# State update over all 128 rows, output products directly behind it, gram products and triangle transposes of both heads in one slot each

## The chip, the cores and the metric

The kernel runs on 1 core of one Trainium2 chip. The metric is the device time of a whole launch in microseconds (us), as the median of the runs. The kernel before takes 3196.33 us (3 runs, 3190.98 to 3197.37).

## The reference, cut to what matters

The program is two transformer layers on an input of (8, 512, 256): softmax attention, an FP4-quantized feed-forward layer, a gated delta rule (a linear attention with a state), and a ternary feed-forward layer. A layer norm follows each. The change lies in the gated delta rule alone, with 8 heads of key and value width 128 and chunks of 64 positions:

```python
tri = tril(k_beta @ k.T * decay, -1)              # per chunk, 64 x 64
Tm = solve_triangular(eye + tri, eye, lower=True)
v_new = Tm @ v_beta;  k_cum = Tm @ (k_beta * exp(g))
def step(S, inp):                                 # chunks in order
    attn = where(keep_low, q_i @ k_i.T * dm_i, 0.0)
    v_n = v_i - kc_i @ S
    out = q_i * exp(g_i) @ S + attn @ v_n
    S = S * exp(g_last) + (k_i * exp(g_last - g_i)).T @ v_n
    return S, out
```

q, k and v come from a projection, a causal convolution over 4 positions and SiLU; a gate z multiplies the normed output. What is computed is the same before and after the change.

## The kernel before

The whole of X stays in SBUF. Four stages run one after the other, with a barrier between them. The third, `delta_rule`, takes two heads (e = 0 and 1) of one sequence at a time: a **pair**. There are 8 sequences of 4 pairs, so 32 pairs. A sequence has 512 positions: 4 tiles t of 128 rows, each tile two chunks of 64 (c = 0 and 1), 8 chunks in all (`NCH`).

The order of the work is written out by hand, and it is the same on every engine. While the state of pair q runs through its chunks, the front of pair f = q + 1 is worked in between. Each pair's turn has 9 **slots** n = 0..8 and then 5 levels of the triangular inverse:

- **p1** (TensorE, line 1966): q and k_cum of chunk n times the state S. VectorE then makes v_n in `V2` (line 1743), and ScalarE copies the part for the output (line 1493).
- `front_early(f, n)` on TensorE and on VectorE: a piece of the next pair.
- **ds** (line 1982): k of chunk n times v_n. It waits for `V2` and for ScalarE's copy. VectorE then updates `S` (line 1759; line 1753 in slot 0), and the next slot's p1 waits for that.
- `front_middle(f, n)` (VectorE only), and `front_late(f, n)` on TensorE: another piece of the next pair.
- **oi** (line 1997), in odd slots: the attention rows times v_n of both chunks of a tile. VectorE adds this to the output `O` (line 1771), and runs its own `front_late` after that.

TensorE's pieces of the front are `keys_in`, `values_in` and `queries_in` (projections, line 1828), `gate_in` (1844), `keys_across` (transposes, 1861), `key_gram` (k times k by chunk, 1876) and `lower_across` (transposes of the 64 x 64 triangles, 1896). On VectorE the pieces are the convolution taps (1537), `keys_to_state` (1551), `keys_to_inverse` (1555), `key_norms` (1559 and 1561, waits for key_gram), `lower` (1582, waits for GpSimd's `key_scales`, whose last instruction is line 1339) and `first_level` (1589 and 1591, waits for lower_across). In the pair that follows the end of a sequence VectorE has the statistics of the layer norm in slot 4 too (`statistics`, 1630 and 1633).

After the levels (lines 2008, 2025 and 2030) TensorE runs `query_gram`, and then for each head the products with the inverse: **vk** (line 2051) and **kc** (line 2058).

An operand's rows and columns decide which part of TensorE's array an instruction uses. The profile prints it as 128*128, 64*128 (64 rows, 128 columns), 128*64 or 64*64. p1, the projections and the 128-wide transposes are 128*128; ds is 64*128, since `KK` and `V2` are taken at the 64 rows of one chunk; oi, lower_across, vk and the levels are 64*64; the grams are 128*64; kc is 64*128. An f32 product shows as two LDWEIGHTS and two MATMUL records.

Of the kernel before, what the change touches and what calls it, by code (L numbers as in the profile page):

```python
# [21 lines left out]
P = 128  # L22
B, N, D = 8, 512, 256
TPS = N // P
# [910 lines left out]
def delta_rule(nc, sems, X, C, prep, ffn, W_qkvz, W_ba, conv_w, dt_bias, A_log, norm_weight, W_out):  # L935
# [19 lines left out]
    with ExitStack() as ctx:  # L955
# [224 lines left out]
        NTm, U, L, ZS = ([sb(f"{n}{e}", [P, TPS, CK]) for e in E2] for n in ("NT", "U", "L", "ZS"))  # L1180
        V2, O = [sb(f"V2{e}", [P, TPS, DK]) for e in E2], [sb(f"O{e}", [P, TPS, DK]) for e in E2]
        S = [sb(f"S{e}", [P, DK]) for e in E2]
# [9 lines left out]
        def per_head(*names):  # L1192
# [14 lines left out]
            sem(n) for n in ("rk_step", "rk_done", "rq_step", "rq_done", "fac_step", "fac_done"))  # L1207
        xt_mm, xt_act, xt_dve, op_mm, y_done, st_done, mv_done, eps_done, rstd_done, ln_done = (
            sem(n) for n in ("xt_mm", "xt_act", "xt_dve", "op_mm", "y_done", "st_done", "mv_done", "eps_done", "rstd_done", "ln_done"))

# [45 lines left out]
        def rows(c):  # L1256
            return slice(c * CK, (c + 1) * CK)
# [8 lines left out]
        with nc.Block() as block:  # L1266
# [263 lines left out]
            def _(dve):  # L1530
# [200 lines left out]
                dve.wait_ge(xt_mm, DC)  # L1731
                nc.vector.tensor_copy(xT[:, 1, :], B_[1][:, :]).then_inc(xt_dve, 1)
                for q in range(-1, PAIRS):
                    f = q + 1
                    for n in range(NCH + 1):
                        for e in E2:
                            m = n
                            if has(q) and 1 <= m < NCH:
                                c, t = m % CPT, m // CPT
                                dve.wait_ge(p1_mm[e], q * RS + m)  # L1740
                                if m == 1:
                                    dve.wait_ge(vnc_done[e], q + 1)
                                nc.vector.scalar_tensor_tensor(V2[e][rows(c), t, :], A_[e][rows(c), 0:DK], cneg[q % 2][rows(c), e, t:t + 1],  # L1743
                                                               VV[e][rows(c), t, :], ALU.mult, ALU.add).then_inc(w_done[e], 1)
# [74 lines left out]
            def _(pe):  # L1819
# [97 lines left out]
                def front_early(f, n):  # L1917

                    if n == 0:
                        keys_in(f, 0, 0)  # L1920
                        keys_in(f, 0, 1)
                    if n == 1:
                        gate_in(f, 0, 0)
                    if n == 2:
                        gate_in(f, 1, 0)
                    if n == 3:
                        gate_in(f, 1, 1)
                    if n == 4:
                        key_gram(f, 1)
                    if n == 5:  # L1930
                        values_in(f, 0, 1)
                    if n == 6:
                        values_in(f, 1, 1)
                    if n == 7:
                        lower_across(f, 1)
                    if n == 8:
                        queries_in(f, 0)

                def front_late(f, n):
# [7 lines left out]
                    if n == 3:  # L1947
                        key_gram(f, 0)
                        keys_across(f, 1)
                    if n == 4:  # L1950
                        values_in(f, 0, 0)
                    if n == 5:
                        values_in(f, 1, 0)
                    if n == 6:
                        lower_across(f, 0)

                x_in(0, 0)
                x_in(0, 1)
                for q in range(-1, PAIRS):
                    f = q + 1  # L1960
                    for n in range(NCH + 1):
# [8 lines left out]
                        for e in E2:  # L1970
                            m = n
                            if has(q) and 0 <= m < NCH:
                                c, t = m % CPT, m // CPT
                                if m == 0:
                                    pe.wait_ge(vnc_done[e], q + 1)
                                    pe.wait_ge(kc_done[e], q + 1)
                                    moving = VV[e][rows(c), t, :]
                                else:
                                    pe.wait_ge(w_done[e], q * RS + m)
                                    pe.wait_ge(o1_done[e], q * RS + m)  # L1980
                                    moving = V2[e][rows(c), t, :]
                                nc.tensor.matmul(A_[e][:, DK:2 * DK], KK[e][q % 2][rows(c), t, :], moving, start=True, stop=True).then_inc(ds_mm[e], 1)  # L1982
                        if has(f):
                            front_late(f, n)
                        for e in E2:
                            m = n
                            if has(q) and 0 <= m < NCH and m % CPT == CPT - 1:
# [7 lines left out]
                                for c in range(CPT):  # L1995
                                    source = VV if t == 0 and c == 0 else V2
                                    last = nc.tensor.matmul(B_[e][rows(c), 0:DK], AT[e][q % 2][rows(c), t, :], source[e][rows(c), t, :],  # L1997
                                                            start=True, stop=True)
                                last.then_inc(oi_mm[e], 1)
                    for l in range(1, LEVELS):  # L2000
                        for e in E2:
# [41 lines left out]
                    if has(f):  # L2043
                        query_gram(f, 0)
                        query_gram(f, 1)
                        for e in E2:
                            pe.wait_ge(u_done[e], f * LEVELS + LEVELS)
                            pe.wait_ge(vv_done[e], f + 1)
                            for t in range(TPS):
                                for c in range(CPT):  # L2050
                                    last = nc.tensor.matmul(F0[e][rows(c), t * P:(t + 1) * P], U[e][rows(c), t, :], VV[e][rows(c), t, :],
                                                            start=True, stop=True)
                            last.then_inc(vk_mm[e], 1)
                            pe.wait_ge(at_done[e], f + 1)
                            pe.wait_ge(ssq_done[e], f + 1)
# [338 lines left out]
```

## Time and profile before

| | us |
|---|---|
| median of the runs | 3196.33 (3190.98 to 3197.37) |
| the profiled execution | 3194.53 |
| its span | 3192.8 |
| TensorE (PE) busy | 2971.4 (93%) |
| VectorE (DVE) busy | 2307.4 (72%) |
| ScalarE (ACT) busy | 1235.1 (39%) |
| GpSimd (POOL) busy | 1020.7 (32%) |
| mean granted TensorE clock | 0.965 |

Busy time says how long at least one instruction of an engine was under way. TensorE's matmuls are pipelined and their ends are modelled, so a busy TensorE may still stand still between two of them. The rows of its weight loads (PEld) have starts that are read directly, and the distance between the starts of two groups shows what a group costs.

### The profile page before, as it was taken

How to read it: one execution, taken by the hardware profiler on the slowest of the kernel's cores; microseconds unless marked ns; L12 is line 12 of the kernel's file. 1: busy time of each engine (PE TensorE's matmuls, PEld its weight loads, DVE VectorE, ACT ScalarE, POOL GpSimd, SP SyncE). 2: the span in 40 equal slices, each digit the busy share in tenths (PEclk: the TensorE clock that was granted, in tenths of full speed). 3: DMA queues.
4: the chain of work that ended last, by engine and by line, in shares of the span. 5: the costliest groups of instructions: out<-in, count | busy, mean ns of one | idle time of the engine just before them, and what ended most of it. 6: DMA issues, size and time to landing. Idle time of an engine off the chain costs nothing. (4 is left out here: it accounts for less than half of the span.)

```text
span 3192.8 us, 82005 instructions
## 1 busy us (share of the span) xinstructions
PE 2971.4 (93%) x33019; PEld 2051.3 (64%) x33019; DVE 2307.4 (72%) x5231; ACT 1235.1 (39%) x2975; POOL 1020.7 (32%) x1495
## 2 busy tenths in 40 slices
PE   6999999679997999999999999999999999999897
PEld 3444444246663777777777777777777777777565
DVE  4666677878874788688678678678678678676566
ACT  2433333323334344344344344344344344342354
POOL 3555455527772222222222222132132132121011
PEclk8999999789997999999999999999999999998899
DMA  2121111000001111001001001001001001000000
GB/s 83 36 58 31 32 31 34 22 1 1 1 1 47 32 41 32 22 19 32 22 18 32 21 19 32 19 21 32 19 21 32 19 22 32 18 18 2 4 25 27
DMA packets 94040, 80.43 MB, mean 25 GB/s; under 512 B 54992, under 2 KB 68320, under 8 KB 93664
## 3 DMA queue, kind: packets, MB, share of 16 engines
q1 hardware_dynamic: 93664, 75.18, 8.7%
q8 instruction: 264, 4.33, 0.6%
q14 instruction: 112, 0.92, 0.1%
HBM read 57.70 MB, written 4.85 MB: 20 GB/s over the span
## 5 line engine op out<-in xcount | busy, mean ns | idle before, releaser
L1828 PE MATMUL gd_bk<-gd_xT,gd_wh 128*128 128x512 f32 x768 | 397.3, 627 | 8.9 <-DVE gd_KE L1555 7.4
L480 DVE TENSOR_REDUCE at_nm<-at_ring 128x2 f32<-128x256 f32 (+3 forms) x256 | 199.2, 821 | 142.9 <-PE at_ring L623 142.9
L1537 DVE SCALAR_TENSOR_TENSOR gd_YK<-gd_bk,gd_cw,gd_YK 128x511 f32<-128x511 f32 (+2 forms) x384 | 283.1, 743 | 11.8 <-ACT gd_YK L1406 6.1
L1506 ACT COPY gd_ZS<-gd_bk 128x256 f32<-128x256 f32 x320 | 119.1, 372 | 318.3 <-PE gd_bk L2008 312.3
L2008 PE MATMUL gd_bk<-gd_L,gd_NT 64*64 64x64 f32 x5120 | 203.7, 223 | 26.5 <-DVE gd_L L1597 25.9
L2008 PEld LDWEIGHTS gd_bk<-gd_L,gd_NT 64*64 64x64 f32 x5120 | 169.2, 134 | 78.8 <-DVE gd_L L1597 40.2
L1595 DVE COPY_PREDICATED gd_U<-gd_mU,gd_bk 128x256 f32<-128x256 int32 x320 | 141.0, 442 | 105.5 <-PE gd_bk L2030 75.1
L1493 ACT COPY gd_O<-gd_bk 64x128 f32<-64x128 f32 x448 | 108.5, 259 | 274.8 <-PE gd_bk L1966 273.9
L2025 PE MATMUL gd_bk<-gd_U,gd_ZS 64*64 64x64 f32 x5120 | 207.6, 220 | 0.1
L302 POOL TENSOR_TENSOR at_PT<-at_PT,at_dm 128x1024 f32<-128x1024 f32 (+3 forms) x128 | 197.8, 1545 | 10.6
L2025 PEld LDWEIGHTS gd_bk<-gd_U,gd_ZS 64*64 64x64 f32 x5120 | 174.6, 135 | 40.8 <-issue 37.1
L1828 PEld LDWEIGHTS gd_bk<-gd_xT,gd_wh 128*128 128x128 f32 x768 | 127.5, 192 | 97.6 <-issue 66.1
L1982 PE MATMUL gd_bk<-gd_V,gd_KK 64*128 64x128 f32 x896 | 167.2, 308 | 20.9 <-DVE gd_V L1743 17.8
L561 PE MATMUL at_ring<-at_QT,at_KT 32*128 32x512 f32 (+3 forms) x1024 | 168.7, 504 | 17.6 <-DVE at_PT L452 12.8
L1982 PEld LDWEIGHTS gd_bk<-gd_V,gd_KK 64*128 64x128 f32 x896 | 123.5, 189 | 94.3 <-DVE gd_V L1743 77.5
L2030 PE MATMUL gd_bk<-gd_ZS,gd_U 64*64 64x64 f32 x4096 | 162.0, 218 | 0.0
L1966 PEld LDWEIGHTS gd_bk<-gd_S,gd_PQ 128*128 128x128 f32 x896 | 127.7, 195 | 52.2 <-issue 37.2
L1966 PE MATMUL gd_bk<-gd_S,gd_PQ 128*128 128x128 f32 x896 | 159.4, 302 | 0.0
L336 ACT ACTIVATE at_PT<-at_ring 128x1024 f32<-128x1024 f32 (+3 forms) x128 | 90.1, 704 | 178.7 <-PE at_ring L561 178.7
L1316 POOL TENSOR_TENSOR gd_zz<-gd_zz,gd_nw_row 128x512 f32<-128x512 f32 x64 | 81.3, 1270 | 240.1 <-ACT gd_zz L1426 240.1
L1771 DVE SCALAR_TENSOR_TENSOR gd_O<-gd_O,gd_tab,gd_bk 128x128 f32<-128x128 f32 x256 | 78.2, 344 | 105.8 <-PE gd_bk L1997 105.1
L1743 DVE SCALAR_TENSOR_TENSOR gd_V<-gd_bk,gd_cneg,gd_VV 64x128 f32<-64x128 f32 x448 | 138.0, 346 | 18.4 <-PE gd_bk L1966 15.0
(354 smaller groups left out, 6772.0 us busy)
## 6 DMA issues: line engine op xcount, KB each, us to landing
gd_wh<-in_L_attn_W_qkvz SPq DMA_DIRECT2D x64, 512.0 KB, 3.7
gd_gb<-gates SPq DMA_DIRECT2D x128, 64.0 KB, 3.3
X<-in_L_attn_x SPq DMA_DIRECT2D x8, 512.0 KB, 8.7
at_QT<-at_QS SPq DMA_DIRECT2D x128, 32.0 KB, 2.0
at_KT<-at_KS SPq DMA_DIRECT2D x128, 32.0 KB, 2.0
at_OC<-at_Ob SPq DMA_DIRECT2D x128, 32.0 KB, 2.0
at_RC<-inverse SPq DMA_DIRECT2D x128, 32.0 KB, 1.8
out_x<-X SPq DMA_DIRECT2D x8, 512.0 KB, 2.9
```

The lines of the kernel that those rows point to most:

```text
L302: nc.gpsimd.tensor_tensor(PT[s % RP][:, 2:GH, 0:n], PT[s % RP][:, 2:GH, 0:n], dm[:, 0:n].unsqueeze(1).broadcast_to([P, 2, n]), ALU.mult).t ...
L480: nc.vector.tensor_reduce(nm[v % 2][:, k, c0:c0 + HS + 1:HS], set_of(s, 2 + p)[:, :, 0:n], AX.X, ALU.max).then_inc(max_done, 1)
L561: last_ = nc.tensor.matmul(set_of(s, p)[:, i, 0:n], KT[lane(u)][r, k * P:(k + 1) * P], QT[lane(u)][r, k * P:W], start=True, stop=True)
L1537: nc.vector.scalar_tensor_tensor(out[:, s:W], bank_[:, 0:W - s], cw[:, j, head(f, e), CONVK - 1 - s:CONVK - s], out[:, s:W], ALU.mult, ALU ...
L1595: last = nc.vector.copy_predicated(U[e][:, :, :], wide(mU[l]), chunks(A_[e], 1))
L1743: nc.vector.scalar_tensor_tensor(V2[e][rows(c), t, :], A_[e][rows(c), 0:DK], cneg[q % 2][rows(c), e, t:t + 1], VV[e][rows(c), t, :], ALU.m ...
L1828: ins = nc.tensor.matmul(out[:, :], wh[e][:, k, col * DK:(col + 1) * DK], xT[:, k, :], start=k == 0, stop=k == DC - 1)
L1966: nc.tensor.matmul(A_[e][:, 0:DK], PQ[e][q % 2][:, m // CPT, m % CPT, :, :].rearrange("p s n -> p (s n)"), S[e][:, :], start=True, stop=Tr ...
L1982: nc.tensor.matmul(A_[e][:, DK:2 * DK], KK[e][q % 2][rows(c), t, :], moving, start=True, stop=True).then_inc(ds_mm[e], 1)
L2008: last = nc.tensor.matmul(A_[e][rows(c), t * CK:(t + 1) * CK], NTm[e][rows(c), t, :], L[e][rows(c), t, :], start=True, stop=True)
L2025: last = nc.tensor.matmul(A_[e][rows(c), (TPS + t) * CK:(TPS + t + 1) * CK], ZS[e][rows(c), t, :], U[e][rows(c), t, :], start=True, stop=True)
L2030: last = nc.tensor.matmul(A_[e][rows(c), t * CK:(t + 1) * CK], U[e][rows(c), t, :], ZS[e][rows(c), t, :], start=True, stop=True)
```

## The change

The state update ds is taken over all 128 rows: the stationary operand is all of `KK[:, t, :]`, and the moving one is `V2[:, t % 2, c, :]`, a tile in which chunk c has its own 64 rows and the other 64 hold zeros that are written once at the start. Slot 0 stays as it was in this respect: `rows(c)` of `KK` and of `VV`. So `V2` becomes [128, 2, 2, 128] and is reused every second tile. The output products oi stand directly behind ds, ahead of front_late. key_gram of head 0 moves from slot 3 (late) to slot 4 (early), just ahead of that of head 1; lower_across of head 0 from slot 6 (late) to slot 7 (early). The products with the inverse run vk of both heads first, and then kc of both.

```diff
-        V2, O = [sb(f"V2{e}", [P, TPS, DK]) for e in E2], [sb(f"O{e}", [P, TPS, DK]) for e in E2]
+        V2, O = [sb(f"V2{e}", [P, 2, CPT, DK]) for e in E2], [sb(f"O{e}", [P, TPS, DK]) for e in E2]
...
 (VectorE, once, behind the first copy of xT)
+                for e in E2:
+                    for c in range(CPT):
+                        last = nc.vector.memset(V2[e][rows(1 - c), :, c, :], 0.0)
+                last.then_inc(v2_clear, 1)
...
-                                nc.vector.scalar_tensor_tensor(V2[e][rows(c), t, :], A_[e][rows(c), 0:DK], cneg[q % 2][rows(c), e, t:t + 1],
+                                nc.vector.scalar_tensor_tensor(V2[e][rows(c), t % 2, c, :], A_[e][rows(c), 0:DK], cneg[q % 2][rows(c), e, t:t + 1],
...
 (TensorE, front_early)
                     if n == 4:
+                        key_gram(f, 0)
                         key_gram(f, 1)
...
                     if n == 7:
+                        lower_across(f, 0)
                         lower_across(f, 1)
...
 (TensorE, front_late)
                     if n == 3:
-                        key_gram(f, 0)
                         keys_across(f, 1)
...
-                    if n == 6:
-                        lower_across(f, 0)
...
 (TensorE, ds)
-                                    moving = VV[e][rows(c), t, :]
+                                    fixed, moving = KK[e][q % 2][rows(c), t, :], VV[e][rows(c), t, :]
...
-                                    moving = V2[e][rows(c), t, :]
-                                nc.tensor.matmul(A_[e][:, DK:2 * DK], KK[e][q % 2][rows(c), t, :], moving, start=True, stop=True).then_inc(ds_mm[e], 1)
-                        if has(f):
-                            front_late(f, n)
+                                    if q == 0 and m == 1:
+                                        pe.wait_ge(v2_clear, 1)
+                                    fixed, moving = KK[e][q % 2][:, t, :], V2[e][:, t % 2, c, :]
+                                nc.tensor.matmul(A_[e][:, DK:2 * DK], fixed, moving, start=True, stop=True).then_inc(ds_mm[e], 1)
...
 (TensorE, oi)
-                                    source = VV if t == 0 and c == 0 else V2
-                                    last = nc.tensor.matmul(B_[e][rows(c), 0:DK], AT[e][q % 2][rows(c), t, :], source[e][rows(c), t, :],
+                                    moving = VV[e][rows(c), t, :] if t == 0 and c == 0 else V2[e][rows(c), t % 2, c, :]
+                                    last = nc.tensor.matmul(B_[e][rows(c), 0:DK], AT[e][q % 2][rows(c), t, :], moving,
                                                             start=True, stop=True)
                                 last.then_inc(oi_mm[e], 1)
+                        if has(f):
+                            front_late(f, n)
...
 (TensorE, between vk and kc)
                             last.then_inc(vk_mm[e], 1)
+                        for e in E2:
                             pe.wait_ge(at_done[e], f + 1)
```

## Rows read from the trace of the kernel before

**Rows 1.** Stretch, length, busy PE, PEld, DVE, ACT, POOL (instructions), TensorE clock, DMA.
```profile
1061.00:2935.00 1874.00, 1817.39 (x25765) 1395.36 (x25764) 1425.30 (x3663) 751.86 (x2048) 445.65 (x878) 0.99 0.09 24
```
**Rows 2.** The same for slots 0 to 8 of single pairs, then the last pair.
```profile
2133.03:2162.49 29.46, 28.92 (x218) 19.56 (x216) 22.88 (x66) 15.05 (x45) 9.39 (x19) 1.00 0.01 3
2259.62:2290.70 31.08, 28.93 (x219) 19.57 (x217) 24.47 (x74) 15.06 (x45) 10.60 (x21) 1.00 0.01 2
2018.60:2051.03 32.43, 30.29 (x218) 20.37 (x216) 24.87 (x74) 15.18 (x45) 10.59 (x21) 0.95 0.01 2
2911.63:2932.19 20.56, 19.82 (x89) 14.68 (x87) 12.04 (x35) 6.06 (x28) 0.33 (x2) 0.59 0.00 0
```
**Rows 3.** Timeline of the weight loads (start, length, line, array part) in slots 2 to 4.
```profile
2141.14 0.52 PEld L1966 LDWEIGHTS gd_bk<-gd_S,gd_PQ 128*128 128x128 f32 x4 [0.17 <-issue]
2141.58 0.97 PEld L1844 LDWEIGHTS gd_bk<-gd_wh,gd_xT 128*128 128x128 f32 x8
2142.68 0.52 PEld L1982 LDWEIGHTS gd_bk<-gd_V,gd_KK 64*128 64x128 f32 x4
2143.32 0.42 PEld L1861 LDWEIGHTS gd_bk<-ident,gd_kT 128*128 128x128 f32 x4
2143.79 0.56 PEld L1966 LDWEIGHTS gd_bk<-gd_S,gd_PQ 128*128 128x128 f32 x4
...
2147.20 0.41 PEld L1997 LDWEIGHTS gd_bk<-gd_V,gd_AT 64*64 64x64 f32 x8 [0.17 <-issue]
2147.78 0.52 PEld L1966 LDWEIGHTS gd_bk<-gd_S,gd_PQ 128*128 128x128 f32 x4 [0.17 <-issue]
```
**Rows 4.** The same view, the products with the inverse and the next keys_in.
```profile
2128.91 0.85 PEld L2051 LDWEIGHTS gd_bk<-gd_VV,gd_U 64*64 64x64 f32 x16
2129.93 0.97 PEld L2058 LDWEIGHTS gd_bk<-gd_U,gd_KE 64*128 64x128 f32 x16 [0.17 <-issue]
2130.97 0.85 PEld L2051 LDWEIGHTS gd_bk<-gd_VV,gd_U 64*64 64x64 f32 x16
...
2133.03 0.30 PEld L1828 LDWEIGHTS gd_bk<-gd_xT,gd_wh 128*128 128x128 f32 x2
```
**Rows 5.** Waits within the stage: who waited for whom, us, times, longest.
```profile
PEld gd_bk L1982 <- DVE gd_V L1743: 77.5, 100, 2.6
...
DVE gd_O L1771 <- PE gd_bk L1997: 105.1, 96, 2.3
```
**Rows 6.** Timeline of VectorE and GpSimd in slots 3 to 7 of one pair.
```profile
2147.68 0.61 DVE L1771 SCALAR_TENSOR_TENSOR gd_O<-gd_O,gd_tab,gd_bk 128x128 f32<-128x128 f32 x2 [1.13 <-PE gd_bk L1997]
2148.80 0.59 DVE L1743 SCALAR_TENSOR_TENSOR gd_V<-gd_bk,gd_cneg,gd_VV 64x128 f32<-64x128 f32 x2
2150.10 0.60 DVE L1759 SCALAR_TENSOR_TENSOR gd_S<-gd_S,gd_egl_row,gd_bk 128x128 f32<-128x128 f32 x2
2151.06 0.42 DVE L1561 TENSOR_REDUCE gd_ssk<-gd_DG 128x4 f32<-128x256 f32 x1
2152.09 0.63 DVE L1743 SCALAR_TENSOR_TENSOR gd_V<-gd_bk,gd_cneg,gd_VV 64x128 f32<-64x128 f32 x2
2153.36 0.60 DVE L1759 SCALAR_TENSOR_TENSOR gd_S<-gd_S,gd_egl_row,gd_bk 128x128 f32<-128x128 f32 x2
2154.41 0.20 POOL L1339 TENSOR_SCALAR gd_cneg<-gd_cc 128x8 f32<-128x8 f32 x1
2155.56 0.85 DVE L1582 SCALAR_TENSOR_TENSOR gd_NT<-gd_bk,gd_cneg,gd_gb 128x64 f32<-128x64 f32 x4
2156.33 0.59 DVE L1743 SCALAR_TENSOR_TENSOR gd_V<-gd_bk,gd_cneg,gd_VV 64x128 f32<-64x128 f32 x2
2157.62 0.59 DVE L1759 SCALAR_TENSOR_TENSOR gd_S<-gd_S,gd_egl_row,gd_bk 128x128 f32<-128x128 f32 x2
```
**Rows 7.** Timeline of TensorE in the same slots, wait in brackets.
```profile
2152.51 0.76 PE L1982 MATMUL gd_bk<-gd_V,gd_KK 64*128 64x128 f32 x4 [0.21 <-DVE gd_V L1743]
...
2280.71 0.76 PE L1982 MATMUL gd_bk<-gd_V,gd_KK 64*128 64x128 f32 x4 [1.82 <-DVE gd_V L1743]
```

More of the change, by code:

```diff
@@ L1207, in delta_rule @@
             sem(n) for n in ("rk_step", "rk_done", "rq_step", "rq_done", "fac_step", "fac_done"))
-        xt_mm, xt_act, xt_dve, op_mm, y_done, st_done, mv_done, eps_done, rstd_done, ln_done = (
-            sem(n) for n in ("xt_mm", "xt_act", "xt_dve", "op_mm", "y_done", "st_done", "mv_done", "eps_done", "rstd_done", "ln_done"))
+        xt_mm, xt_act, xt_dve, op_mm, y_done, st_done, mv_done, eps_done, rstd_done, ln_done, v2_clear = (
+            sem(n) for n in ("xt_mm", "xt_act", "xt_dve", "op_mm", "y_done", "st_done", "mv_done", "eps_done", "rstd_done", "ln_done", "v2_clear"))
         w_fc, w_proj = ffn
```

## The prediction

> **What bounds the kernel now.** I read the busy time by stretch first. The stage that the change touches takes 1874 us of the span, and in it TensorE is busy for 97% and VectorE for 76% [rows 1]. Busy TensorE time isn't the same as a working array, so the second view is the start times of its weight loads. In them the reader is to see two kinds of steps. Where one group follows another on the same part of the array, it starts after the time of its own records: p1 (4 records) to gate_in is 0.44 us, keys_across to p1 is 0.47 us, so a 128-column record costs about 0.107 us [rows 3]. Where the part of the array changes, there is more. Gate_in's 8 records are worth 0.86 us and ds starts after 1.10 (0.24 more); ds's 4 records are worth 0.43 us and keys_across starts after 0.64 (0.21 more); oi, whose two chunks run beside each other and which is worth 0.43 too, is followed by p1 after 0.58 (0.15 more) [rows 3]. I call this a **switch** and take 0.2 us for it. The third view is the waits: TensorE's loads wait for V2 77.5 us in all, and VectorE waits 105.1 us for oi [rows 5]. So TensorE bounds the slots, with VectorE's loop over the state close behind it in slots 4 to 7.
>
> **The slots: switches.** I count the changes of array part through slots 0 to 8 of a pair with a front, from the order in the code. Before, ds (64*128) stands between 128*128 work, and oi (64*64) too. By slot 0 to 7 there are 2, 4, 2, 5, 3, 4, 3 and 4 changes, 27 in all. After, ds belongs to the 128*128 work except in slot 0, where it keeps its 64 rows; oi's entry and exit stay; head 0's gram and triangle transposes share the entry and exit of head 1's. That gives 2, 2, 0, 2, 2, 2, 0 and 4, so 14. Thirteen go, at 0.2 us: 2.6 us per pair. ds itself costs the same: p1 loads 128 rows and ds 64, and four records of either are 0.43 us [rows 3].
>
> **The slots: waits.** A wait that goes or comes is worth as much as a switch, so I walk the pair that starts at 2133.03 and takes 29.46 us to the first level [rows 2]. All times are from that start. Up to p1 of slot 4 nothing stops TensorE for more than 0.1 us in such a walk. It started its load at 14.75 and its stream 0.11 later [rows 3]; seven switches (1.4) and head 0's gram (0.43) are gone from ahead of it, so now 13.0. From here on VectorE decides:
> - Slot 4. V2 starts at about 13.6, behind the pieces of slot 3. Key_norms of head 0 now waits for the moved gram: p1 ends at 13.4, switch and 8 pairs of 0.053 bring 14.05, and about 0.2 for the result makes 14.25. Before, VectorE had it at once. S starts 0.8 later, at 15.05. VectorE's next V2 follows S by 1.99 us (2150.10 to 2152.09), so at 17.05, and ds of slot 5 can stream 0.53 us behind that (2152.51 for its load, 0.11 for the load itself), at 17.6 [rows 6, 7]. TensorE is through with p1 and values_in at 17.25: it waits 0.35 us.
> - Slot 5. S comes 1.27 us after V2 [rows 6], at 18.3, and O directly behind it. O no longer waits for oi, since oi now follows ds; that is where VectorE's 105.1 us go [rows 5]. `lower` of head 0 needs GpSimd's scales: they end 3.55 us after the second reduction starts (2151.06 to 2154.61) [rows 6]; this reduction is at 16.0, so 19.6. p1 of slot 6 streams at 19.65.
> - Slot 6. V2 follows `lower` by 0.77 us, at 20.4, S follows V2 by 1.29, at 21.65 [rows 6], and the next p1 streams 0.5 us after S starts, at 22.15. TensorE ended ds at 21.35. Before, lower_across of head 0 stood here and hid this; now 0.8 us are a wait. This is the price of moving it.
> - From p1 of slot 7 to the first level only TensorE counts: p1 0.43, switch, both triangle transposes 0.86, switch, ds 0.43, switch, oi 0.43, switch 0.15, queries_in 0.11 + 1.71, switch: 4.8 us. End at 26.95.
>
> So 29.46 − 26.95 = **2.5 us per pair**, for 31 pairs with both a state loop and a front: 77.5 us. The bounds: with no waits left at all it is 13 x 0.24 = 3.1 us (96 us). With VectorE's steps taken one by one at full length rather than by starts (its records overlap by some hundredths each) I come to 1.7 us (53 us). I take 2.5, since it rests on start-to-start distances.
>
> **vk and kc.** Before, the two heads take 4.12 us from the first vk to keys_in (2128.91 to 2133.03), as vk 1.02 and kc 1.04, twice [rows 4]. Sixteen records of either are worth 0.86. After: 2 x 0.86 + 0.17 + 2 x 0.86 + 0.18 = 3.8 us. kc now waits for all of vk, but what it needs from VectorE (`ssq`) comes at the same time as before or sooner than TensorE gets there. Gain 0.35 us x 32 = 11 us; 0 if a wait fills it.
>
> **What costs nothing.** The four memsets stand on VectorE while TensorE does its first projections; uncovered they'd be about 1 us, once (four times at most 0.3, by rows of like size [rows 6]). The reuse of V2 after two tiles adds no wait, as oi of that tile was issued ahead of the p1 that V2 waits for. The last pair has no front: its chain runs p1, V2, ds, S with TensorE waiting at each step at a clock of 0.59 [rows 2], so a switch is under a wait there; I give it 0, and the first pair, which has no ds, 0 with ±1 us. Queues of SP and GpSimd are passed by nothing.
>
> **The clock.** In pairs behind the end of a sequence VectorE has the statistics in slot 4, and ds of slot 5 waits 1.82 us [rows 7]. These 7 pairs take 31.08 us at a granted clock of 1.00, or 32.43 at 0.95 where it falls (four of the seven fell) [rows 2]. This wait grows by the 0.35 us above less nothing. If all seven fall, 3 x 1.4 = 4 us more; I put 5 us.
>
> **Sum.** 77.5 + 11 − 5 = 84 us. The profiled execution took 3194.5; 3110.7 after. The median is 1.8 us above the profiled one, so **3112 us**, 2.6% faster.
>
> One rule of the skill speaks against the change. Rows 3 show that p1, with 128 rows, starts its four loads 0.11 us apart and gate_in follows at once, so a full-height load is hidden behind the product ahead of it. The Trainium skill (TensorE: Matmul & The Clock Gate, Part 3, The mechanism) says of packed products that a weight load overlaps with running matmuls only where its row group differs; a ds over all 128 rows would differ from nothing. By that rule the loads of ds would show, and rival 3 gives the time; the trace doesn't bear it out.
>
> **Rivals.**
> 1. VectorE's loop bounds more of the slots, and only 1.7 us per pair come: 53 + 11 − 5 = 59 us, **3137**. For it: three waits in a row from slot 4 on hang on it. Against: starts, not lengths, are what the rows give.
> 2. The step of 0.2 us at ds isn't from the array part but from its wait for VectorE, so ds keeps it. Then only the moves of oi, gram and triangles count: 5 switches, 1.0 us, 31 + 11 = 42 us, **3154**. Against: keys_across to p1, where p1 waits for VectorE's S in the same way, has no such step [rows 3].
> 3. A full-height load of ds isn't hidden: 4 x 0.107 = 0.43 us in each of 7 slots, 3.0 us in 31 pairs, 93 us, so **3205**.
> 4. Slower: the clock. TensorE's wait at slot 5 and its new one at slot 6 lie close together, and the clock falls to the lower level (1.2 of 2.4 GHz) in every pair, from ds of slot 5 to the first level. Its stream there is 7.3 us, which doubles; the 0.8 us wait hides a part: 6.5 x 31 = 201 us, **3313**. It decides from 2.5 us a pair on. For it: after 1.82 us of waiting the clock did fall in four of seven. Against: a fall cost 1.35 us (32.43 against 31.08), and the ordinary pairs with their wait of 0.2 us show 1.00 [rows 2, 7]. The Trainium skill (TensorE: Matmul & The Clock Gate, Part 1) has the half clock as the state that idling brings back, which the clock of 0.59 in the last pair agrees with [rows 2].
> 5. More than forecast: the waits at slots 5 and 6 don't come, 96 + 11 = 107, **3089**.
>
> **How the numbers follow.** Forecast 0.60, rival 1 0.19, rival 5 0.09, rival 2 0.06, rival 3 0.03, rival 4 0.03. The range reaches into rivals 1 and 5 and leaves out 2 to 4: 3088 to 3145. About 0.2% (6.4 us) is what a measurement can tell from no change. Faster are the forecast and rivals 1, 2 and 5, 0.94; slower 3 and 4, 0.05, with little between.
>
> **What would show it.** ds in rows as 128*128, and 0.44 us between its load and the next 128*128 group; slots of an ordinary pair in 27.0 us; a new wait of about 0.8 us of p1 for S ahead of slot 7, and 0.3 for V2 at slot 5; hardly any wait of line 1771; vk to keys_in in 3.8 us. Wrong would be a step of 0.64 behind a 128*128 ds, slots over 28 us, or a clock under 0.98 in ordinary pairs.

## The result and the profile after

The changed kernel takes **3104.74 us** (median of 4 runs, 3101.75 to 3115.75) against 3193.65 us for the kernel before, run beside it on the same chips (median of 4). The ratio is **0.9728**, with a 95% interval of 0.97 to 0.9756. The profiled execution took 3101.75 us with a span of 3100.0 us; before it was 3194.53 and 3192.8. The medians are 88.9 us apart and the two profiled executions 92.8 us; I had forecast 84.

Stretches first. The first row is the part of the stage that rows 1 showed, the others are slots 0 to 8 of three pairs: an ordinary one, and two behind the end of a sequence. The columns are as in rows 1.

```profile
1055.00:2842.00 1787.00, 1728.68 (x25789) 1373.19 (x25788) 1429.34 (x3668) 749.19 (x2052) 450.21 (x886) 1.00 0.09 25
2309.64:2336.83 27.19, 26.68 (x218) 19.11 (x216) 23.48 (x67) 15.03 (x45) 9.76 (x21) 1.00 0.01 4
2660.20:2688.77 28.57, 26.68 (x218) 19.11 (x216) 25.14 (x76) 15.08 (x45) 10.95 (x23) 1.00 0.01 3
2200.29:2230.54 30.25, 28.36 (x218) 19.95 (x216) 25.45 (x76) 15.21 (x45) 10.95 (x23) 0.94 0.01 3
```

An ordinary pair's slots went from 29.46 to 27.19 us [rows 2], so 2.27 us less; the forecast said 26.95. VectorE's busy time in them hardly changed (22.88 before, 23.48 now), but it is now 86% of the slots instead of 78%. A pair behind the end of a sequence gained 2.5 us where the clock stayed at 1.00 (28.57 against 31.08 us). Of the seven pairs behind the end of a sequence one shows a fallen clock (0.94) in this execution, where four did before.

The last pair, which has no front beside it, ran at a granted clock of 1.00 this time, 15.45 us against 20.56 at 0.59 before [rows 2]:

```profile
2821.05:2836.50 15.45, 13.40 (x86) 9.65 (x84) 11.04 (x35) 5.95 (x28) 0.43 (x3) 1.00 0.00 1
```

Next the weight loads of TensorE in slots 2 to 4 (start, length, line, part of the array).

```profile
2317.41 0.53 PEld L1968 LDWEIGHTS gd_bk<-gd_S,gd_PQ 128*128 128x128 f32 x4
2317.86 0.97 PEld L1848 LDWEIGHTS gd_bk<-gd_wh,gd_xT 128*128 128x128 f32 x8
2318.76 0.53 PEld L1986 LDWEIGHTS gd_bk<-gd_V,gd_KK 128*128 128x128 f32 x4
2319.20 0.47 PEld L1865 LDWEIGHTS gd_bk<-ident,gd_kT 128*128 128x128 f32 x4
...
2321.71 0.41 PEld L1999 LDWEIGHTS gd_bk<-gd_V,gd_AT 64*64 64x64 f32 x8
2322.29 0.42 PEld L1865 LDWEIGHTS gd_bk<-ident,gd_kT 128*128 128x128 f32 x4 [0.17 <-issue]
2322.68 0.53 PEld L1968 LDWEIGHTS gd_bk<-gd_S,gd_PQ 128*128 128x128 f32 x4
```

ds (line 1986) is 128*128 now. Gate_in's 8 records take 0.90 us to the start of ds instead of 1.10, and ds's 4 records 0.44 us to keys_across instead of 0.64 [rows 3]. Behind oi the 0.58 us stay, as they were before.

The products with the inverse and the next keys_in, same view:

```profile
2359.99 1.72 PEld L2055 LDWEIGHTS gd_bk<-gd_VV,gd_U 64*64 64x64 f32 x32
2361.88 1.86 PEld L2063 LDWEIGHTS gd_bk<-gd_U,gd_KE 64*128 64x128 f32 x32 [0.17 <-issue]
2363.81 0.30 PEld L1832 LDWEIGHTS gd_bk<-gd_xT,gd_wh 128*128 128x128 f32 x2
```

From vk to keys_in it is 3.82 us instead of 4.12 [rows 4].

The waits of the stage (us in total, times, longest). No line for O (now 1775) waiting for oi is left in this view, where 105.1 us stood before [rows 5]. TensorE's loads of ds (1986) wait less for V2, 53.4 us instead of 77.5. Those of p1 (1968) wait more for S, 26.4 us instead of 11.1:

```profile
PEld gd_bk L1986 <- DVE gd_V L1747: 53.4, 69, 2.5
...
PEld gd_bk L1968 <- DVE gd_S L1763: 26.4, 65, 0.7
```

The line of before for p1 is this one:

```profile
PEld gd_bk L1966 <- DVE gd_S L1759: 11.1, 34, 0.3
```

And the walk of slots 4 to 7, for the pair that starts at 2309.64 (all engines, start, length, line):

```profile
2322.37 0.60 DVE L1775 SCALAR_TENSOR_TENSOR gd_O<-gd_O,gd_tab,gd_bk 128x128 f32<-128x128 f32 x2
2322.88 0.68 DVE L1555 TENSOR_TENSOR gd_KE<-gd_bk,gd_tab 128x512 f32<-128x512 f32 x1
2323.48 0.59 DVE L1747 SCALAR_TENSOR_TENSOR gd_V<-gd_bk,gd_cneg,gd_VV 64x128 f32<-64x128 f32 x2
2324.06 0.42 DVE L1559 TENSOR_TENSOR gd_DG<-gd_bk,gd_identc 128x256 f32<-128x256 f32 x1
...
2324.93 0.61 DVE L1763 SCALAR_TENSOR_TENSOR gd_S<-gd_S,gd_egl_row,gd_bk 128x128 f32<-128x128 f32 x2
...
2326.26 1.02 PE L1832 MATMUL gd_bk<-gd_xT,gd_wh 128*128 128x512 f32 x2
2326.94 0.63 DVE L1747 SCALAR_TENSOR_TENSOR gd_V<-gd_bk,gd_cneg,gd_VV 64x128 f32<-64x128 f32 x2
2327.35 0.57 PEld L1986 LDWEIGHTS gd_bk<-gd_V,gd_KK 128*128 128x128 f32 x4 [0.90 <-DVE gd_V L1747]
...
2328.21 0.60 DVE L1763 SCALAR_TENSOR_TENSOR gd_S<-gd_S,gd_egl_row,gd_bk 128x128 f32<-128x128 f32 x2
...
2329.49 0.86 DVE L1582 SCALAR_TENSOR_TENSOR gd_NT<-gd_bk,gd_cneg,gd_gb 128x64 f32<-128x64 f32 x4 [0.17 <-POOL gd_cneg L1339]
...
2330.27 0.59 DVE L1747 SCALAR_TENSOR_TENSOR gd_V<-gd_bk,gd_cneg,gd_VV 64x128 f32<-64x128 f32 x2
...
2331.55 0.59 DVE L1763 SCALAR_TENSOR_TENSOR gd_S<-gd_S,gd_egl_row,gd_bk 128x128 f32<-128x128 f32 x2
2331.94 0.75 PE L1968 MATMUL gd_bk<-gd_S,gd_PQ 128*128 128x128 f32 x4 [0.44 <-DVE gd_S L1763]
```

| from the pair's start, us | forecast | measured |
|---|---|---|
| V2 of slot 4 | 13.6 | 13.84 |
| key_norms of head 0 | 14.25 | 14.42 |
| S of slot 4 | 15.05 | 15.29 |
| V2 of slot 5 | 17.05 | 17.30 |
| S of slot 5 | 18.3 | 18.57 |
| `lower` of head 0 | 19.6 | 19.85 |
| V2 of slot 6 | 20.4 | 20.63 |
| S of slot 6 | 21.65 | 21.91 |
| p1 of slot 7 | 22.15 | 22.30 |
| first level | 26.95 | 27.19 |

The whole error of the walk comes in at V2 of slot 4 and is 0.24 us at the end too. (The forecast for p1 of slot 7 is for its products and the 22.30 is the start of its load, 0.11 us ahead of them; like for like that error is 0.26.) VectorE's own queue sets the start of V2 there: O and KE of slot 3 stand directly ahead of it in the first two lines, with no wait between.

Both waits that the forecast named are there. Values_in starts at 2326.26, its two products are worth 0.85 us (the forecast's 1.71 is for four), and the load of ds starts at 2327.35 and takes 0.11 until it can stream: 0.35 us of wait for V2 at slot 5, as forecast. At slot 7, p1 streams 0.5 us behind S, 22.41 us into the pair, and ds of slot 6, whose products start at 21.25, had ended at 21.68: 0.73 us, where I had 0.8.

### The profile page after: what moved, and what is told of

The parts are those of the page before. It is cut to its first block and busy times, and to the rows that moved or that the text cites. A ratio compares the mean times of both kernels' runs of the same rounds, so it can differ in the third digit from the quotient of the medians.

```text
span 3100.0 us, 82009 instructions
## 1 busy us (share of the span) xinstructions
PE 2875.9 (93%) x33019; PEld 2026.8 (65%) x33019; DVE 2311.7 (75%) x5235; ACT 1230.7 (40%) x2975; POOL 1021.2 (33%) x1495
## 5 line engine op out<-in xcount | busy, mean ns | idle before, releaser
L561 PE MATMUL at_ring<-at_QT,at_KT 32*128 32x512 f32 (+3 forms) x1024 | 167.3, 496 | 18.5 <-DVE at_PT L452 13.6
L1986 PE MATMUL gd_bk<-gd_V,gd_KK 128*128 128x128 f32 x896 | 150.3, 290 | 14.6 <-DVE gd_V L1747 13.0
L1986 PEld LDWEIGHTS gd_bk<-gd_V,gd_KK 128*128 128x128 f32 x896 | 121.5, 190 | 61.2 <-DVE gd_V L1747 53.4
L1968 PE MATMUL gd_bk<-gd_S,gd_PQ 128*128 128x128 f32 x896 | 144.8, 284 | 12.5 <-DVE gd_S L1763 12.5
L299 POOL TENSOR_SCALAR_AFFINE_SELECT at_PT<-at_PT 128x256 f32<-128x256 f32 x128 | 54.6, 427 | 297.8 <-ACT at_PT L336 297.2
L338 ACT ACTIVATE at_PT<-at_PT 128x1024 f32<-128x1024 f32 (+3 forms) x128 | 94.3, 737 | 139.8 <-DVE at_PT L452 139.8
```

What stands on the lines that cost most here:

```text
L561: last_ = nc.tensor.matmul(set_of(s, p)[:, i, 0:n], KT[lane(u)][r, k * P:(k + 1) * P], QT[lane(u)][r, k * P:W], start=True, stop=True)
L1968: nc.tensor.matmul(A_[e][:, 0:DK], PQ[e][q % 2][:, m // CPT, m % CPT, :, :].rearrange("p s n -> p (s n)"), S[e][:, :], start=True, stop=Tr ...
L1986: nc.tensor.matmul(A_[e][:, DK:2 * DK], fixed, moving, start=True, stop=True).then_inc(ds_mm[e], 1)
```

## The experiments

The kernel before ran again beside each variant (medians 3192.35 to 3194.97 us), so times are compared through their ratios to it. Each variant's median is of 4 or 5 runs. "Slots" is the length of slots 0 to 8 of an ordinary pair, read from the profile.

| kernel | slots, us | median, us | ratio (95%) |
|---|---|---|---|
| before | 29.46 | 3193.65 | 1 |
| changed | 27.19 | 3104.74 | 0.9728 (0.97 to 0.9756) |
| e1: changed, ds over 64 rows | 27.78 | 3127.32 | 0.9797 (0.9784 to 0.9811) |
| e2: before, ds over 128 rows alone | 28.93 | 3176.47 | 0.9953 (0.9941 to 0.9966) |
| e3: changed, head 0's triangles back | 26.79 | 3099.02 | 0.9709 (0.9695 to 0.9722) |
| e4: changed, both heads' triangles in slot 6 | 26.99 | 3098.24 | 0.9707 (0.9694 to 0.972) |
| e5: changed, head 0's gram back | 27.37 | 3117.22 | 0.9759 (0.9745 to 0.9773) |
| e6: changed, oi back behind front_late | 28.56 | 3153.92 | 0.9882 (0.9869 to 0.9896) |
| e7: changed, vk and kc by head again | 27.19 | 3122.24 | 0.9764 (0.974 to 0.9789) |
| e8: changed and three edits | 26.40 | 3069.42 | 0.9615 (0.9602 to 0.9628) |
| e9: changed, statistics in slot 8 | 27.19 | 3095.85 | 0.9699 (0.9686 to 0.9713) |
| e10: e6, VectorE's O behind its front_late | 27.76 | 3123.93 | 0.9782 (0.9768 to 0.9795) |
| e12: e8, `lower` of head 1 behind S | 26.46 | 3074.77 | 0.963 (0.9617 to 0.9643) |

**e1: the rows of ds undone.**

```diff
-fixed, moving = KK[e][q % 2][:, t, :], V2[e][:, t % 2, c, :]
+fixed, moving = KK[e][q % 2][rows(c), t, :], V2[e][rows(c), t % 2, c, :]
```

> The changed kernel with one thing undone: ds takes 64 rows again (KK and V2 at the rows of its chunk), everything else as changed. Theory (each change of array part costs 0.2 us): 8 changes more per pair with a front, 1.6 us, of which up to 0.4 lies under the waits at slots 5 and 6: 1.2 to 1.6 us, so an ordinary pair's slots take 28.4 to 28.8 us instead of 27.2, and the time is 37 to 50 us above the changed kernel, about 3142 to 3155. Rival (the step of 0.2 us at ds came from its wait for VectorE): no change, about 3105.

Measured: 22.6 us slower, slots 0.59 us longer, which is less than the 37 to 50 us and the 1.2 to 1.6 us expected. The price of one switch is as forecast. In the weight loads of e1's slot 2, gate_in, ds, keys_across:

```profile
1174.95 0.97 PEld L1848 LDWEIGHTS gd_bk<-gd_wh,gd_xT 128*128 128x128 f32 x8
1176.04 0.52 PEld L1986 LDWEIGHTS gd_bk<-gd_V,gd_KK 64*128 64x128 f32 x4
1176.68 0.42 PEld L1865 LDWEIGHTS gd_bk<-ident,gd_kT 128*128 128x128 f32 x4
```

1.09 and 0.64 us, where the changed kernel has 0.90 and 0.44: the same code, no wait shown in either, only the rows differ. So the shape makes the step, and rival 2 falls. But eight such switches come to 0.59 us, not 1.6. The expectation allowed 0.4 us of cover by waits; at 0.2 us a switch it is about 1.

**e2: the rows of ds alone.** The kernel before with V2, the memsets and the operands of ds as changed, nothing moved.

> The kernel before with one part of the change alone: ds over all 128 rows with the zero-padded V2; order of the work as before. Theory (switches): 9 of the 27 changes of array part go, 1.8 us per pair, 56 us at most; some of it turns into waits for VectorE in slots 4 to 6. 35 to 56 us faster than before: ratio 0.982 to 0.989. Rival (the gain is in the order, oi directly behind ds and the shared slots): under 15 us. Rival (a full-height load is not hidden): slower than before by up to 93 us.

Measured: 0.53 us per pair and a ratio of 0.9953, 15 us (17 by the medians). That misses my 35 to 56 us and lies at the edge of "the gain is in the order". The weight loads of one pair of e2 show where it ends; the first lines are slot 1, the last are slots 4 and 5:

```profile
1176.71 0.52 PEld L1988 LDWEIGHTS gd_bk<-gd_V,gd_KK 128*128 128x128 f32 x4
1177.15 0.97 PEld L1848 LDWEIGHTS gd_bk<-gd_wh,gd_xT 128*128 128x128 f32 x8
...
1186.68 0.56 PEld L1988 LDWEIGHTS gd_bk<-gd_V,gd_KK 128*128 128x128 f32 x4 [0.22 <-DVE gd_V L1747]
...
1187.97 0.57 PEld L1970 LDWEIGHTS gd_bk<-gd_S,gd_PQ 128*128 128x128 f32 x4 [0.52 <-DVE gd_S L1763]
...
1189.99 0.57 PEld L1988 LDWEIGHTS gd_bk<-gd_V,gd_KK 128*128 128x128 f32 x4 [1.22 <-DVE gd_V L1747]
```

ds to gate_in is 0.44 us: a load of full height is hidden as p1's are, and rival 3 falls. ds of slot 3 starts 0.54 us sooner than before in its pair (11.79 against 12.33 us from its start), and this lead never grows again. p1 of slot 3 already waits 0.22 us for S, and from there on what TensorE saves it waits for V2 and S. TensorE's loads wait 107.6 us for the two in the stage of e2 and 88.6 before. VectorE's loop over the state is the second bound, and it was already there: VectorE still stands at O for oi (94.6 us).

**e3 and e4: the triangle transposes.** e3 puts those of head 0 back, e4 puts both heads' into slot 6.

```diff
 (front_early, n == 7)
-                        lower_across(f, 0)
                         lower_across(f, 1)
 (front_late)
+                    if n == 6:
+                        lower_across(f, 0)
```

> The changed kernel with lower_across of head 0 back in slot 6, behind ds. Theory (p1 of slot 7 waits for VectorE's S anyway, so the transposes and their two switches are covered there, and slot 7 is rid of 0.43 us): slots 26.7 us instead of 27.2, 12 to 16 us faster than the changed kernel, about 3090. Rival (only the number of switches counts): one or two switches more, 6 to 12 us slower, about 3114.

> The changed kernel with lower_across of both heads in slot 6, behind ds. Theory: two switches and 0.86 us leave slot 7; in slot 6 head 1's transposes wait for `lower` of head 1 and push p1 of slot 7 by 0.2 us, and ds of slot 7 then waits 0.5 us for V2: net 0.35 to 0.5 us a pair, 11 to 16 us faster than the changed kernel, about 3091. Rival (switch count alone): 2 fewer switches and nothing else, 0.4 us. Rival (the clock falls more often behind the wait at slot 7): slower than the changed kernel.

Measured: 0.40 and 0.20 us a pair less. For e3 that is near the 0.5 expected of the slots: this part of the change costs time. e4 misses its 0.35 to 0.5. The weight loads of e3 in slots 6 and 7:

```profile
1186.28 0.54 PEld L1900 LDWEIGHTS gd_bk<-gd_identc,gd_NT 64*64 64x64 f32 x16
1186.89 0.52 PEld L1969 LDWEIGHTS gd_bk<-gd_S,gd_PQ 128*128 128x128 f32 x4
1187.53 0.55 PEld L1900 LDWEIGHTS gd_bk<-gd_identc,gd_NT 64*64 64x64 f32 x16
1188.15 0.53 PEld L1987 LDWEIGHTS gd_bk<-gd_V,gd_KK 128*128 128x128 f32 x4
```

p1 of slot 7 starts 22.39 us into its pair against 22.30 in the changed kernel: the transposes and both their switches fit into the time for which p1 waited for S anyway. ds of slot 7 comes 1.26 us behind it instead of 1.75. In e4 there is more in that place than the wait can hide:

```profile
1190.04 0.52 PEld L1970 LDWEIGHTS gd_bk<-gd_S,gd_PQ 128*128 128x128 f32 x4
1190.98 0.57 PEld L1988 LDWEIGHTS gd_bk<-gd_V,gd_KK 128*128 128x128 f32 x4 [0.42 <-DVE gd_V L1747]
```

p1 of slot 7 starts 22.86 us into its pair, 0.57 later than in the changed kernel and not the 0.2 I expected, and ds behind it waits 0.42 us for V2.

As times, both are only 6 to 7 us faster than the changed kernel, and the intervals overlap. For e4, 31 x 0.2 makes that; for e3 31 x 0.4 would make 12. Its pairs behind the end of a sequence gained only 0.17 us (28.40 against 28.57). In e3's profile three of them take 30.0 us and not 28.4, where the changed kernel's has one such pair, and these two more are 3.3 us of it.

**e5: the gram of head 0 back in slot 3.**

```diff
 (front_early, n == 4)
-                        key_gram(f, 0)
                         key_gram(f, 1)
 (front_late, n == 3)
+                        key_gram(f, 0)
                         keys_across(f, 1)
```

> The changed kernel with key_gram of head 0 back in slot 3, behind oi and ahead of keys_across. Theory (VectorE's loop decides slots 4 to 6, and key_norms of head 0 would no longer wait, but p1 of slot 4 comes 0.6 us later and V2 with it): S of slot 4 0.3 us later, slots 27.5 us, 9 us slower than the changed kernel. Rival (switches alone, one more of 0.17 us, under no wait): 5 us slower. Rival (the moved gram delays VectorE more than it saves): faster than the changed kernel.

Measured: slots 27.37, so 0.18 us and 5.6 us in 31 pairs. That size lies by the rival's 5 us rather than by my 9. The path is nearer to what I expected: V2 of slot 4 waits for p1 and comes 14.18 us into the pair instead of 13.84, S of slot 4 comes 0.20 us later, and so does all that follows.

```profile
1180.78 0.60 DVE L1747 SCALAR_TENSOR_TENSOR gd_V<-gd_bk,gd_cneg,gd_VV 64x128 f32<-64x128 f32 x2 [0.26 <-PE gd_bk L1968]
```

The time is 10 us by the ratios; five of its seven pairs behind the end of a sequence show the fallen clock, four more than the changed kernel's one.

**e6: oi back behind front_late.** The switches stay the same in number.

```diff
                                 nc.tensor.matmul(A_[e][:, DK:2 * DK], fixed, moving, start=True, stop=True).then_inc(ds_mm[e], 1)
+                        if has(f):
+                            front_late(f, n)
...
                                 last.then_inc(oi_mm[e], 1)
-                        if has(f):
-                            front_late(f, n)
```

> The changed kernel with oi back behind front_late; the number of changes of array part stays the same as in the changed kernel. Theory (VectorE's queue stands at O until oi, and its loop over S is delayed by it in slots 1, 3 and 5): the waits of VectorE for oi come back to 60 us or more, and slots take 27.6 to 28.2 us instead of 27.2, 13 to 30 us slower. Rival (only switches count): no change within 3 us.

Measured: 1.37 us a pair and 49 us. This is the largest part of the change, and more than the 13 to 30 us expected. The waits of VectorE in e6's stage bring back 69.8 us for O:

```profile
DVE gd_O L1775 <- PE gd_bk L2001: 69.8, 97, 2.3
```

**e10: the same, but VectorE's update of O moved too.** e6 with `front_late(f, n)` ahead of the update of O in VectorE's block; TensorE's order is e6's.

> The kernel with oi back behind front_late (28.57 us for the slots, 3154 us) plus one edit: VectorE's update of O stands behind its own front_late, so that its queue does not wait for oi. TensorE's order is untouched. Theory (what oi's place is worth is VectorE's wait): most of the 1.39 us a pair comes back, slots 27.2 to 27.7 us, 3105 to 3125. Rival (it is TensorE's order itself, the switches or what stands between ds and the next p1): stays at 28.3 or more, about 3150.

Measured: slots 27.76, 0.80 of the 1.37 us back, so at least that much of what oi's place is worth is VectorE's queue standing at O. The other 0.57 us come in between slots 5 and 6. Up to ds of slot 5 e10 is within 0.05 us of the changed kernel (17.75 against 17.70 us into the pair); V2 of slot 6 comes 0.57 us later, at 21.19 instead of 20.62. These are e10's TensorE and VectorE there:

```profile
1184.17 1.12 PE L1832 MATMUL gd_bk<-gd_xT,gd_wh 128*128 128x512 f32 x2 [0.23 <-DVE gd_KE L1555]
1185.22 0.65 PE L2001 MATMUL gd_bk<-gd_V,gd_AT 64*64 64x128 f32 x8
1185.32 0.86 DVE L1582 SCALAR_TENSOR_TENSOR gd_NT<-gd_bk,gd_cneg,gd_gb 128x64 f32<-128x64 f32 x4 [0.69 <-POOL gd_cneg L1339]
1185.81 0.71 PE L1968 MATMUL gd_bk<-gd_S,gd_PQ 128*128 128x128 f32 x4
1186.10 0.59 DVE L1777 SCALAR_TENSOR_TENSOR gd_O<-gd_O,gd_tab,gd_bk 128x128 f32<-128x128 f32 x2
1186.61 0.59 DVE L1747 SCALAR_TENSOR_TENSOR gd_V<-gd_bk,gd_cneg,gd_VV 64x128 f32<-64x128 f32 x2
```

What ends last ahead of V2 is VectorE's own queue. `lower` waits for GpSimd's scales and starts as early as in the changed kernel (19.90 against 19.85 us). There O stands ahead of it, under that wait; here O stands behind it, and V2 can start 0.51 us later for it. So what ends last here is the price of e10's own edit, and the 0.57 us can't be put down to TensorE's order.

TensorE's order has an effect too, hidden behind this one. Values_in of head 1 waits for VectorE's KE (its loads wait 13.2 us in all in the stage of e10, 13.1 in e6 and before, and no such wait is in the changed kernel); with oi ahead of it, TensorE does oi in that time. The products of p1 of slot 6 start 20.39 us into the pair in e10 and 19.95 in the changed kernel. Where V2 waits for p1, as in slot 2 of the changed kernel, it starts 0.53 us behind p1's load (7.78 and 8.31 us into the pair). By that V2 of slot 6 would come at 20.92, 0.3 us late: an estimate, as no run shows it alone.

**e7: vk and kc by head again.** The added `for e in E2:` removed.

> The changed kernel with vk and kc of one head directly behind each other again. Two switches more per pair, nothing waits there: first vk to keys_in 4.12 us instead of 3.82, 0.3 us in 32 pairs, 10 us slower. Rival (these products are hidden behind VectorE's `new_values`): no change.

Measured: the distance from vk to keys_in is 4.12 us again and the pair 0.31 us longer, 10 us in all, as expected. The time rose by 17.5 us in the median (11.5 by the ratios), and its five runs reach from 3101.95 to 3124.7. Most of the rest is the clock. These are e7's slots of two pairs behind the end of a sequence:

```profile
1290.09:1318.67 28.58, 26.69 (x218) 19.13 (x216) 25.02 (x75) 15.08 (x45) 10.76 (x22) 1.00 0.01 3
1520.39:1550.64 30.25, 28.36 (x219) 20.00 (x217) 25.24 (x75) 15.19 (x45) 10.76 (x22) 0.94 0.01 2
```

Six of its seven such pairs are of the second kind, 1.67 us longer at a granted clock of 0.94. The changed kernel had one: 5 x 1.67 = 8.4 us.

**e9: the statistics out of slot 4.**

```diff
-                        if n == 4 and ends_seq(q - 1):
+                        if n == 8 and ends_seq(q - 1):
                             statistics(seq(q - 1))
-                        if n == 8 and ends_seq(q - 1):
-                            normalize(seq(q - 1))
...
+                        if l == 5 and ends_seq(q - 1):
+                            normalize(seq(q - 1))
```

> The changed kernel with the layer norm's statistics in slot 8 instead of slot 4, and normalize in level 5. Theory (in the 7 pairs behind the end of a sequence VectorE's statistics hold up ds of slot 5 by 1.6 us, and behind that wait the granted clock falls in some of them, 1.65 us each): all 31 pairs at 27.2 us, no pair at 28.6 or 30.2; 10 us plus 1.65 us for each fall that is gone, so 10 to 20 us faster than the changed kernel, and the runs closer together than its 3102 to 3116. Rival (the instructions cost the same in slot 8): no change.

Measured: 9 us faster by the ratios (0.9699 against 0.9728; the intervals overlap), just under the 10 to 20 expected, all 30 pairs whose starts I read between 27.18 and 27.36 us and none with a fallen clock, as here the pair behind the first sequence:

```profile
1283.75:1310.94 27.19, 26.68 (x218) 19.11 (x216) 23.67 (x68) 15.03 (x45) 9.61 (x20) 1.00 0.02 5
```

So the wait made by VectorE's statistics is what the clock falls behind. The runs (3090 to 3101) still lie 10 us apart, against 14 for the changed kernel, so the clock of these pairs isn't all of the scatter. The last pair is part of it: its granted clock was 0.81 in this profile, 1.00 in that of the changed kernel and 0.53 in e6's.

**e8: three edits together.** e3's and e9's, and ds of slot 0 over 128 rows too:

```diff
 (ScalarE, behind its copies of kc)
+                            act.wait_ge(vnc_done[e], f + 1)
+                            last = nc.scalar.copy(V2[e][rows(0), 0, 0, :], VV[e][rows(0), 0, :])
                             last.then_inc(kc_done[e], 1)
 (TensorE, ds of slot 0)
-                                    fixed, moving = KK[e][q % 2][rows(c), t, :], VV[e][rows(c), t, :]
+                                    fixed, moving = KK[e][q % 2][:, t, :], V2[e][:, 0, 0, :]
```

> The changed kernel with three more edits. (1) lower_across of head 0 back in slot 6. (2) ds of slot 0 over 128 rows too, its moving operand copied by ScalarE into V2's padded tile at the end of the pair. (3) The layer norm's statistics leave slot 4 for slot 8, and normalize goes to level 5. Theory: (1) 0.39 us in 31 pairs; (2) two switches less, 0.4 us for TensorE up to slot 3, of which VectorE's loop gives back 0 to 0.3 from slot 4 on; (3) 1.4 us in 7 pairs, and fewer falls of the clock behind the wait of slot 5. Together 15 to 35 us faster than the changed kernel, 3070 to 3090. Rival (VectorE's loop takes (2) back whole, and (3)'s instructions delay the levels as much as they did slot 4): 5 to 12 us faster only.

Measured: **3069.42 us, 3.85% faster than before** and 35 us faster than the changed kernel. The pair behind a sequence's end is as short as any:

```profile
1285.61:1312.01 26.40, 26.33 (x219) 19.17 (x217) 23.39 (x67) 15.18 (x47) 9.61 (x20) 1.00 0.03 6
```

The time is at the good edge of the range expected. Against e3's 26.79 us the two switches of slot 0 bring 0.39, the whole 2 x 0.2: all later starts in the pair move up with them (p1 of slot 4 from 13.04 to 12.64 us), so VectorE's loop gives nothing back. TensorE is busy for 26.33 of the 26.40 us.

**e12: `lower` of head 1 behind S in slot 6**, and the first tap of head 0's values in slot 8.

> The combined version (slots 26.40 us, 3069 us) with VectorE's order changed in two places: `lower` of head 1 behind the update of S in slot 6 instead of ahead of it, and the first tap of the values of head 0 in slot 8 instead of slot 6. Theory (p1 of slot 7 waits for S, and S for `lower`): p1 of slot 7 comes 0.3 us sooner, slots 26.1 us, 9 us faster. Rival (V2 of slot 7 is then late, or slot 8's taps hold up the first level): no change or slower.

Measured: slots 26.46 and 5 us slower, which is the rival (the intervals of the two ratios overlap a little). p1 of slot 7 starts at 22.01 us as in e8, because with head 0's transposes back in slot 6 it was TensorE's own queue that it followed, not S. VectorE now waits there instead:

```profile
1187.43 0.61 DVE L1764 SCALAR_TENSOR_TENSOR gd_S<-gd_S,gd_egl_row,gd_bk 128x128 f32<-128x128 f32 x2 [0.45 <-PE gd_bk L1988]
```

And with `lower` of head 1 done later, its transposes in slot 7 wait for it, which is where the 0.06 us come in:

```profile
1188.86 0.54 PEld L1901 LDWEIGHTS gd_bk<-gd_identc,gd_NT 64*64 64x64 f32 x16 [0.18 <-DVE gd_NT L1584]
```

## Why the prediction was right, and which of its terms were not

The mechanism held: switches went, VectorE's loop over the state took part of what they gave, and the walk found how much. That the total comes as close is in part luck: the slots and the products with the inverse gave less than forecast, and the clock and a sooner start gave more.

- **The switches.** Right in kind and in size: 0.20 us off at each side of ds, shown by e1 against the changed kernel with nothing else altered.
- **The walk.** 2.5 us a pair forecast, 2.27 measured. The mis-sized term is the start of V2 in slot 4, 13.6 instead of 13.84, from the part of the walk that I gave without rows; each later step kept its distance within 0.1 us. The wait of key_norms for the moved gram, which I put ahead of S, is at most some hundredths: key_norms starts 0.58 us behind V2, against 0.52 before (2148.80 to 2149.32).
- **vk and kc.** 0.35 forecast (its own figures, 4.12 and 3.8, give 0.32); 0.30 measured, and shown by e7.
- **The wait at slot 7.** It came where it was forecast, ahead of p1 of slot 7, with 0.73 us for 0.8. (TensorE's idle time reads 0.44 us, as its modelled ends reach into the gap.) e3 shows the price of moving the transposes from there: 0.40 us a pair that this part of the change gives away.
- **The worth of each part.** Here the text misleads, though its walk is right. It names 13 switches at 0.2 us as the gain and gives the place of oi nothing of its own beyond VectorE's waits. By single undoing the rows are worth 0.59 us, oi's place 1.37, the gram 0.18, the triangles −0.40: 1.74 of the 2.27 us together. The rows alone (e2) brought 0.53, so they are worth about the same with the rest of the change and without it: most of their switches are under waits for VectorE either way. Why the single parts fall 0.5 us short of the whole wasn't tested, as no run undoes two parts together. The changed kernel's waits of 0.35 and 0.73 us could hide part of any one undoing.
- **The clock.** I said that the wait at slot 5 behind the statistics would grow by 0.35 us, and set 5 us of loss for falls in all seven pairs. TensorE's wait there was 1.67 us, where it was 1.82 before [rows 7], and there were fewer falls, one against four. With one at 0.90 before, which took 33.69 us and which I had counted like the others, the fewer falls gave 5 us of gain. The variants that leave the statistics in slot 4 had one to six in their profiles (e7 six, with the same wait of 1.67 us), so the number isn't shown to be a property of the change.
- **Where 92.8 us come from.** 24 ordinary pairs x 2.27 = 54.5; the seven others 22.6 (2.5 us each, and 5.1 the clock); 32 x 0.30 = 9.6 for vk and kc: 86.7. The remaining 6 us are in no term of the forecast. The stage begins 3.9 us sooner in this execution (1005.8 against 1009.7 us for its first transposes), where nothing was changed. The last pair took 15.45 instead of 20.56 us at a clock of 1.00, and what follows it took 3.1 us longer, so 2.0 us of gain; I had given it 0, at a clock of 0.59. That clock was between 0.53 and 1.00 in the profiles of the variants.
- **Luck.** Without the clock the parts give 54.5 + 17.5 + 9.6 = 81.6 us, where the forecast had 77.5 + 11 = 88.5. The clock and the sooner start gave about 11 us in the profiled execution, where the forecast took 5 off. The two errors have opposite signs, and so 84 us lie near the 88.9 between the medians.
- **Small slips.** The terms written down from p1 of slot 7 to the first level add to 4.92 us and not to 4.8 (measured from the products of p1: 4.78). Rivals 3 and 4 have 0.06 together, not 0.05. Rival 5 leaves out the 5 us for the clock.
- **The memsets.** 1.36 us of VectorE once, with VectorE idle for 4.66 us behind them; they cost nothing, as forecast.
- **Rivals.** Rival 1 (VectorE's loop bounds more) has the mechanism that e2 shows, but not its size. Rivals 2 and 3 fall by e1 and e2. Rival 4 (the clock at half in every pair) did not come: ordinary pairs show 1.00.

## What to carry to other kernels

Where products of different row and column extents alternate, look at the distances between weight-load starts: a product on half the rows that stands between full ones can cost two steps of 0.2 us. Zero padding to full height took them away here, and the product's own four records took no longer (0.43 to 0.44 us). But count what the second engine of the loop allows, since nine steps less gave 0.53 us a pair here and not 1.8. Put the product that another engine's queue stands waiting for directly where its inputs are ready: undoing this cost 1.37 us a pair. And leave work that can stand under an unavoidable wait there: moved out of it to save a step, it cost 0.40 us a pair.

## What the runs showed of the hardware that I had not expected

- With the same code, only the rows of one operand pair different, the distance from ds to the next full-size group is 0.44 or 0.64 us, and the one ahead of it 0.90 or 1.09.
- Behind a wait of TensorE for V2 in slot 5 (1.82 us before the change, 1.67 after it), the granted clock of the pair's slots was 0.94 in one of seven pairs of the changed kernel (in one to six of seven in the variants with the statistics in slot 4), at 1.2 to 1.7 us each. Before it was 0.95 in three and 0.90 in one, which cost 2.6 us. With the statistics moved it fell in none (e8, e9, e12).
- The last pair, in which TensorE waits at most steps, had a granted clock of 0.53 (e6), 0.58 (e1), 0.59 (before), 0.81 (e9) or 1.00 (changed, e2, e8, e10) and took 22.0 us from its first load to its last oi in e6 and 15.8 in the changed kernel.
